# PSUM waits per tile at layer begins, and a re-cut first weight load, in a one-core FFN / S4D / FFN kernel

## The reference, cut to what matters

```python
def _L0_ffn_ref(x, w1_w, w1_s, w2_w, w2_s, h1_w, h1_s, h2_w, h2_s, w3_w, w3_s):
    h = jax.nn.silu(_tlin(x, w1_w, w1_s)) * _tlin(x, w2_w, w2_s)
    h = jax.nn.gelu(_tlin(h, h1_w, h1_s), approximate=False)
    h = jax.nn.gelu(_tlin(h, h2_w, h2_s), approximate=False)
    return _tlin(h, w3_w, w3_s)
...
x = x + 0.5 * _L0_ffn_ref(_layernorm(x), ...)
x = x + _L0_attn_ref(_layernorm(x), ...)
x = x + 0.5 * _L0_ffn_ref(_layernorm(x), ...)
```

## Time and profile before

| what | value |
|---|---|
| median of the runs | 1329.17 us (1328.3 to 1329.56) |
| the profiled execution's own time | 1328.43 us |
| its span, first to last instruction | 1326.6 us |
| what lies around the span | 1.8 us |
| TensorE busy | 1315.0 us, 99% of the span |
| VectorE, ScalarE, GpSimd busy | 65%, 56%, 30% |
| mean granted clock of TensorE | 0.998 |

### The profile page before, as it was taken

One profiled execution on the slowest core, in us unless ns is written; L12 is line 12 of the kernel. 1 busy time (PEld: TensorE's weight loads), 2 busy tenths in 40 slices (PEclk: granted clock), 3 DMA queues, 4 the chain that ended last, 5 costly groups with the idle time before them and its releaser, 6 DMA issues.

```text
span 1326.6 us, 18338 instructions
## 1 busy us (share of the span) xinstructions
PE 1315.0 (99%) x7278; PEld 670.0 (51%) x7278; DVE 867.3 (65%) x1703; ACT 746.3 (56%) x1201; POOL 402.9 (30%) x394
## 2 busy tenths in 40 slices
PE   8999999999999999999999999999999999999998
PEld 3454454644545445455454554545545455454544
DVE  5277767423455876978779787787877874454633
ACT  4665457645356566673765736657467464545432
POOL 6721377600012422623226233261432600001000
PEclk9999999999999999999999999999999999999999
DMA  8310000000010000000100000000010002231400
GB/s 309 135 40 9 8 1 17 1 9 9 0 56 9 8 10 1 16 1 1 16 1 17 9 9 17 17 8 17 8 17 17 8 17 72 56 104 34 157 1 18
DMA packets 44701, 41.88 MB, mean 32 GB/s; under 512 B 32704, under 2 KB 41408, under 8 KB 41920
## 3 DMA queue, kind: packets, MB, share of 16 engines
q1 hardware_dynamic: 44320, 40.54, 10.2%
q10 hardware_dynamic: 288, 0.10, 0.0%
HBM read 28.57 MB, written 4.19 MB: 25 GB/s over the span
## 4 chain that ended last, share of the span: by engine, by line
PE 96%; ACT 1%; DVE 1%; DMA 0%; issue 0%; DVEq 0%
PE psf L1345 65%; PE psf L1333 17%; PE psf L1357 8%; PE pss L1408 2%; PE pss L1418 2%; PE pss L1398 2%; PE pss L1373 1%; PE pss L1388 1%; ACT g L1154 1%; DMA scr<-sc 0%; DVE arena L804 0%; ACT psf L1115 0%; ACT hab L1108 0%; DVE arena L801 0%; DVE xr L657 0%
## 5 line engine op out<-in xcount | busy, mean ns | idle before, releaser
L1345 PE MATMUL psf<-hab,wall 128*128 128x512 f16 x4096 | 890.9, 379 | 2.4 <-DVE ht L640 0.9
L1345 PEld LDWEIGHTS psf<-hab,wall 128*128 128x128 f16 x4096 | 399.3, 98 | 483.4 <-issue 5.2
L1115 ACT ACTIVATE psf<-psf,scf 128x512 f32<-128x512 f32 x256 | 168.7, 659 | 430.0 <-PE psf L1345 429.9
L628 DVE SCALAR_TENSOR_TENSOR hab<-psf,hab 128x512 f16<-128x512 f32 x256 | 175.3, 687 | 317.4 <-ACT hab L1108 317.1
L1333 PE MATMUL psf<-h,wall 128*128 128x512 f16 x1024 | 232.9, 381 | 0.7 <-ACT h L1119 0.7
L1333 PEld LDWEIGHTS psf<-h,wall 128*128 128x128 f16 x1024 | 99.8, 98 | 117.1 <-issue 1.9
L1108 ACT ACTIVATE hab<-psf 128x512 f16<-128x512 f32 x256 | 152.8, 597 | 8.1
L972 POOL TENSOR_SCALAR rs<-mv 128x4 f32<-128x4 f32 x16 | 3.1, 194 | 468.4 <-DVE mv L671 468.4
L640 DVE SCALAR_TENSOR_TENSOR ht<-psf,scf,sil 128x512 f32<-128x512 f32 x128 | 95.0, 749 | 72.4 <-PE psf L1333 69.9
L1098 ACT ACTIVATE sil<-psf,scf 128x512 f32<-128x512 f32 x128 | 87.1, 685 | 90.6 <-PE psf L1333 88.5
L628 DVE SCALAR_TENSOR_TENSOR hab<-ht,hab 128x512 f16<-128x512 f32 x128 | 118.1, 931 | 3.0
(11 more groups left out here) (131 smaller groups left out, 904.3 us busy)
## 6 DMA issues: line engine op xcount, KB each, us to landing
arena<-wh SPq DMA_DIRECT2D x8, 1024.0 KB, 5.6
g<-wh SPq DMA_DIRECT2D x6, 1024.0 KB, 8.6
out<-xr SPq DMA_DIRECT2D x15, 256.0 KB, 2.2
xr<-x SPq DMA_DIRECT2D x7, 512.0 KB, 5.1
arena<-w SPq DMA_DIRECT2D x3, 1024.0 KB, 5.5
g<-w SPq DMA_DIRECT2D x2, 1024.0 KB, 7.0
xr<-wh SPq DMA_DIRECT2D x2, 1024.0 KB, 9.6
g<-w SPq DMA_DIRECT2D x2, 512.0 KB, 6.7
```

The lines of the kernel that those rows point to most:

```text
L628: e.scalar_tensor_tensor(out=hab[:, buffer(p), m, 1, :], in0=source(p), scalar=2.0 ** E2 if l else 1.0, in1=hab[:, buffer(p), m, 0, :], op ...
L1115: e.activation(bank, bank, ACT.Gelu, scale=scf[:, 2 + l, m:m + 1]).then_inc(s_gelu, 1)
L1345: ins = e.matmul(bank[:, :], WH[:, l, m // 2, k, ms], hab[:, buffer(p), k, part, :], start=(k == 0 and part == 0), stop=(k == KH - 1 and p ...
```

## The change

Three things are changed.

1. **Bank waits at the begin of a hidden layer.** `pe_program` asked for all three banks ahead of the first matmul. Now it asks for the bank of tile `m` directly ahead of tile `m`'s matmuls. This holds for 32 layer begins.
2. **The first piece of the gated weights.** It is still loaded in two transfers of the same size, but each now holds the columns of two of the four tiles for both `l` and both `k` (rows of 1 KB where they were 4 KB). Three casts wait for the first transfer's half and the second's: ScalarE casts `l` = 0 of the first half, GpSimd `l` = 1 of the first half and then both `l` of the second. `s_cast2` counts to 3 where it counted to 1, and TensorE waits for 1 ahead of tile 0, for 2 and 3 ahead of tile 2.
3. **Order at the start.** The constants `cs` are issued by SyncE's queue between the rows of `x` and the weights, where ScalarE's queue issued them first. VectorE normalises the first rows ahead of the four multiplications of the scales, where it did so behind them.

```diff
--- before.py
+++ after.py
@@ -346,6 +346,7 @@
         win16 = cs[:, C_WC:C_END].bitcast(F16).rearrange("p (h n) -> p h n", h=2)
         w16 = wts[:, :, :].rearrange("p k n -> p (k n)").bitcast(F16).rearrange("p (h k n) -> p h k n", h=2, k=2)
         stage = g3[:, :, :, :].rearrange("p c n d -> p (c n d)")
+        first_w = stage[:, 0:2048].rearrange("p (l k n) -> p l k n", l=2, k=2)
         pm = [[stage[:, 1024 * (2 * e + n):1024 * (2 * e + n + 1)].bitcast(F16).rearrange("p (o d g x) -> p o d g x", o=4, d=8, g=4)
                for n in range(2)] for e in range(2)]
         again = [arena[:, 2048 * i:2048 * (i + 1)] for i in range(2)]
@@ -694,6 +695,7 @@
 
                 w.wait_ge(s_again[i % 2], 16 * (i // 2 + 1))
                 w.wait_ge(*cast_of(i))
+                w.wait_ge(s_cast2, 3)
                 w.wait_ge(s_same, i)
                 e.scalar_tensor_tensor(
                     out=junk, in0=again[i % 2], scalar=0.0, in1=pieces[i][1], op0=ALU.add, op1=ALU.not_equal,
@@ -907,11 +909,11 @@
             e.memset(one[:, :], 1.0).then_inc(s_init, 1)
             e.memset(hab[:, 1, 0, 0, :], 0.0).then_inc(s_init, 1)
             sums(0)
+            norm_first()
             w.wait_ge(s_scl, 16)
             for n, e2 in enumerate((-E0, E1 - E0, -E1, -E2)):
                 e.tensor_scalar(scf[:, n, :], scr[:, n, :], 2.0 ** e2, None, ALU.mult).then_inc(s_sc, 1)
             w.wait_ge(s_sc, 4)
-            norm_first()
             for k in range(2):
                 low_first(k)
 
@@ -998,7 +1000,7 @@
             def powers():
                 yield At(mark["z"][0])
                 w.wait_ge(s_cast, len(ACT_CASTS))
-                w.wait_ge(s_cast2, 1)
+                w.wait_ge(s_cast2, 3)
                 for o in range(4):
                     ch.done(e.memset(stage[:, 1024 * o:1024 * (o + 1)], 0.0))
                 pmark["zero"] = now["slot"], ch.n
@@ -1051,8 +1053,11 @@
             e.memset(half[:, :], -0.5).then_inc(s_halved, 1)
             scales_of(0)
             w.wait_ge(s_nrm, TPC)
+            w.wait_ge(s_w0[0], 16)
+            e.tensor_copy(W12[:, 0, 1, :, 0:D], first_w[:, 1, :, 0:D]).then_inc(s_cast2, 1)
             w.wait_ge(s_w0[1], 16)
-            e.tensor_copy(wall[:, 1024:2048], stage[:, 1024:2048]).then_inc(s_cast2, 1)
+            for l in range(2):
+                e.tensor_copy(W12[:, 0, l, :, D:2 * D], first_w[:, l, :, D:2 * D]).then_inc(s_cast2, 1)
             cast(1)
             w.wait_ge(s_ks, 16)
             for n, _ in enumerate(rates(ch)):
@@ -1084,7 +1089,7 @@
 
             def cast_first():
                 w.wait_ge(s_w0[0], 16)
-                e.activation(wall[:, 0:1024], stage[:, 0:1024], ACT.Copy).then_inc(s_cast, 1)
+                e.activation(W12[:, 0, 0, :, 0:D], first_w[:, 0, :, 0:D], ACT.Copy).then_inc(s_cast, 1)
 
             def cast(p):
                 w.wait_ge(s_st[p % STAGES], st_count(p))
@@ -1259,7 +1264,6 @@
 
             w.wait_ge(s_init, 2)
             e.activation(one2[:, :], hab[:, 1, 0, 0, 0:1], ACT.Silu)
-            e.dma_start(cs[:, 0:C_DA], cst[:, 0:C_DA]).then_inc(s_cst, 16)
             e.dma_start(scr[:, :, :].rearrange("p a k -> p (a k)"), sc).then_inc(s_scl, 16)
             cast_first()
             for k in range(2):
@@ -1322,7 +1326,9 @@
                 w.wait_ge(*cast_of(m // 4))
                 for l in range(2):
                     bank = main(bank_use(i, "up", 2 * m + l))
-                    if l:
+                    if m > 1:
+                        w.wait_ge(s_cast2, l + 2)
+                    elif l:
                         w.wait_ge(s_cast2, 1)
                     for k in range(2):
                         for part in range(2):
@@ -1446,8 +1452,9 @@
             for i in range(PASSES):
                 for l in range(2):
 
-                    banks = [main(bank_use(i, "hid", KH * l + m)) for m in range(EARLY)]
+                    banks = []
                     for m in range(EARLY):
+                        banks.append(main(bank_use(i, "hid", KH * l + m)))
                         hidden(i, l, m, banks[m], range(KH - 2))
                     for m in range(EARLY):
                         hidden(i, l, m, banks[m], (KH - 2,))
@@ -1503,8 +1510,11 @@
 
             e.dma_start(xr[:, 0:2, :], xv[:, 0:2, :]).then_inc(s_x0a, 16)
             e.dma_start(xr[:, 2:4, :], xv[:, 2:4, :]).then_inc(s_x[0], 16)
+            e.dma_start(cs[:, 0:C_DA], cst[:, 0:C_DA]).then_inc(s_cst, 16)
             for h in range(2):
-                e.dma_start(stage[:, 1024 * h:1024 * (h + 1)], w12[:, 1024 * h:1024 * (h + 1)]).then_inc(s_w0[h], 16)
+                e.dma_start(first_w[:, :, :, D * h:D * (h + 1)],
+                            w12[:, 0:2048].rearrange("p (l k n) -> p l k n", l=2, k=2)[:, :, :, D * h:D * (h + 1)]
+                            ).then_inc(s_w0[h], 16)
             e.dma_start(small[:, 0:320], ks).then_inc(s_ks, 16)
             for p in range(1, STAGES):
                 load_piece(p)
```

## The result

The changed kernel takes 1322.51 us (median of five, 1322.29 to 1322.89), the kernel before 1329.17 beside it (five here too, 1327.44 to 1329.56): 6.7 us less, a ratio of 0.9955 with the 95% interval [0.9942, 0.9968]. Forecast were 1324.3 us and a range of 1322.4 to 1327.0. The span fell from 1326.6 to 1320.7 us, by 5.9; forecast were 4.9.

The account below looks back on a forecast made before the run. TensorE, busy 1315.0 of 1326.6 us, was taken as the bound, so only late matmul starts counted. Layer begins 4.2 plus start 0.7 made 4.9 us less: 1329.17 to 1324.3, range 1322.4 to 1327.0.

Parts of the forecast that it names:

- the late begins: Hidden-layer begins where TensorE starts late: 0.56 and 0.65 us, seven layer 0 begins together 2.13, one layer 1 0.78.
- Part 1: Bank waits at hidden-layer begins: they go with the per-tile order, 4.2 us less in sum.
- the low part of tile 7: In the layer 1 begun near 1049 us, TensorE would wait for this VectorE part to 1058.48; 0.2 us comes back.
- The rival that VectorE gives half back: Layer begins: half of the 4.2 us returns as waits for VectorE; 2.8 us less in all, 1326.4, 15%.
- The 0.24 us of pass 0: Pass 0's first hidden layer: a bank wait hidden in the weight loads, next load at 26.14 instead of 25.90.
- Part 2: The start: earlier normalisation brings the up matmuls forward; 0.7 us, the middle between 0.48 and 0.96.
- the 0.96: At the start, VectorE normalises ahead of the scales; transposes, high part and first up matmul each come 0.96 us earlier.
- the clock, to which I gave 5% for staying up: At the start, a shorter pause ahead of the up matmuls keeps TensorE's clock up: 6.6 us less, 1322.6, 5%.
- this very case: At the start, TensorE's clock stays up: 6.6 us less, 1322.6, 5%; with the runs' spread, the range's lower end 1322.4.
- the clock's return: At the start, return to full clock moves with the up matmuls (0.96 us gained, 1324.0) or stays at 13.6 (0.48, 1324.5).
- The cover: ScalarE's first cast, cut to 512 columns, about 0.6 us: weights may land at 8.4; beyond, every 0.1 us costs 0.1.
- rival of late weights: ScalarE's first cast: weights land 1 to 2 us over 8.4, 1325.5, 7%; or at 14.5, 1330.2, 3% for over 1329.2.

Follow-up runs that it names:

- the start alone: The changed kernel with all three banks asked for at once again, so only the changes at the start remain: 1326.57 us, ratio 0.9981 to the kernel before.

## Why the prediction was right or wrong

*What bounds the kernel, and reading start times.* Right. Seven of the late begins, those of 0.3 us, had no idle time in the profile, and they were real: together 2.1 us. Going by the 1.5 us that the profile puts down to L640 and L628, one would have missed over half.

*Part 1, 4.2 us.* Right to a few tenths in the profiles; in the medians the bank waits alone brought 5.3. The 1.1 more would fit the wait at pass 0's layer begin (below), but no trace of a timed execution shows it there. From 430 us on the two profiles are 3.9 apart in the sum of late groups; all named begins are at 3.45. Of the wait that I expected back at the low part of tile 7 (0.2), 0.11 shows. The rival that VectorE gives half back is out by the bank waits alone.

*The 0.24 us of pass 0* were misread. They are the lateness of a weight load, and those run a matmul ahead. The 64 up matmuls from 10.70 took 15.58 us with 0.38 for the last, so that one started at 25.90 and the next was due at 26.12; the first hidden matmul started at 26.17, 0.05 late. As a term it was wrong too: in five of the seven profiles with three banks at once it is 1.1 to 1.3 us. I took the layer begins and the start for separate terms, and this begin belongs to both.

*Part 2, 0.7 us.* Too small: 2.2 us in the spans, which more than makes up the 1.0 by which they miss the forecast. In the two profiles compared the shift of the first up matmul, forecast at 0.96, was 1.19, since the rows of x landed sooner as well. But the 0.96 was the size of one launch: the old start began its up matmuls anywhere from 9.89 to 11.11, the new one from 9.42 to 9.86. And the clock, to which I gave 5% for staying up, falls in 2 of 31 only. I had reasoned that the pause holds the same transposes. The pause was the wrong measure: from the first profile of before to that of the changed kernel it grew (1.51 and 1.74 us idle ahead of the transposes), and in the second the clock stayed up. That the result lies within the range is owed to its lower end, which was taken from this very case, 6.6 us less; that the whole measured 6.7 bears out the sum and not its terms, since the bank waits alone brought 5.3. The Trainium skill ("TensorE: Matmul & The Clock Gate", What's actually happening) says that the activity window is free-running; the executions agree, in that the same kernel falls in some and not in others. I drew from it only where the clock's return would lie, and not that whether it falls at all can differ from launch to launch.

*The cover: ScalarE's cast and the landing of the weights.* The weights landed at 8.06 in the first profile, within the limit of 8.4, and no rival of late weights came in the medians. In one of five profiles they came at 8.55, beyond it: there the cast ended at 9.18, behind the transposes, and the first up matmul came at 9.81, 2.72 behind the normalisation's begin where it is 2.54 elsewhere. That is the 0.1 for each 0.1 us beyond the limit, 0.2 us here. The cut, meant to cover the gain of the start, is worth nothing that shows: with the old one the start is as early.

*The constants' move, put at nothing.* Wrong in kind: it removes the wait for the scales alone, and brings x sooner. The order on VectorE, to which I gave the 0.96, is the second remedy for the same wait.

*The sum.* 4.9 forecast; 6.7 between the medians, 5.9 between the spans. Right in direction and nearly all of part 1; the start, mis-sized, was 0.7 in the sum and 2.2 in the spans.

What stays open: why the landing of the first rows and of the first weights varies from launch to launch, by 0.8 and 1.4 us, and how much of the spread between executions at the same clock is due to it. That spread is large with three banks at once (1325.93 to 1329.43 us for the 11 executions of the start alone, all at 0.999 or 1.000) and small with the waits per tile (1321.67 to 1323.72 for the 23 of all such kernels at 0.999 or 1.000). That fits waits which appear in some launches, and was not tried. Nor is shown that the earlier up matmuls are what keeps the clock up; the profiles fit it, 14 of them.

## What to carry to other kernels

On an engine with overlapping instructions, look for lost time in start times, not in idle time: a group that takes longer than its count times its pitch has waited, whatever the busy share says. Ask for a buffer directly ahead of its first use, never for several at once; the last of three banks was wanted 5 us after the first, and the wait for it cost 0.3 to 1.3 us at the begins where it was late. And test parts of a change together as well as apart, and compare the profiled execution's time with the median before a sum rests on its trace: here the two parts measured 3.0 and 5.3 us alone and at most 6.7 together, and the one trace of the start alone, taken 1.6 us above its median, would have suggested that it is worth next to nothing.

## What the runs showed of the hardware that was not expected

- The same kernel has the clock fall at its start in some launches and not in others: for certain in 34 of 51 for the kernel before. One profile tells which of the two it saw, not which is usual; the mean clock of every execution tells that in most cases, but a profile at 0.999 can be of either kind, since the clock also falls behind the last matmul.
- A 16 KB transfer took 4.1 to 6.0 us to land as the second of its queue (seven profiles), and 2.5 to 2.8 as the first (seven profiles).
- The same start varies from launch to launch: in four profiles of kernels with the old start and 14 matmuls on the zero tile, the first up matmul came at 9.89, 10.33, 10.70 and 11.11 us.
- A low part of VectorE with both inputs outside PSUM took 2.06 to 2.38 us when it began within 0.4 us of a cast of weights on GpSimd (0.68 in other places of pass 0), and 2.55 beside GpSimd's products; those that read PSUM kept to 0.68 beside such products.
